# Later heads of the first group on a spare bank, second group's staged reads first, mirrored tokens and late sums moved

## What is computed

```
h = tokens(x)             # |FFT| of (poly+gauss), sigmoid mask, soft minimum
xn = layernorm(h)
q, k, v = xn @ Wq, xn @ Wk, xn @ Wv        # 8 heads of 64
attn = sigmoid(q k^T * 8)                   # keys and queries of one signal
h = h + relu((attn v) @ Wo)
y = layernorm(h)
h = h + shared_mlp(y) + top2_of_4_experts(y)
```

## Time and profile before

| | us |
|---|---|
| three runs | 173.07, 173.97, 174.40 (median 173.97) |
| the profiled execution, whole | 172.75 |
| its span, first to last instruction | 170.9 |
| PE busy | 152.8 (89% of the span) |
| ACT busy | 113.2 (66%) |
| DVE busy | 109.2 (64%) |
| POOL busy | 53.1 (31%) |
| TensorE's mean granted clock | 0.97 of full |

### The profile page before, as it was taken

One profiled execution on the slowest core, in us unless ns is written; L12 is line 12 of the kernel. 1 busy time (PEld: TensorE's weight loads), 2 busy tenths in 40 slices (PEclk: granted clock), 3 DMA queues, 4 the chain that ended last, 5 costly groups with the idle time before them and its releaser, 6 DMA issues.

```text
span 170.9 us, 6658 instructions
## 1 busy us (share of the span) xinstructions
PE 152.8 (89%) x2826; PEld 92.0 (54%) x2826; DVE 109.2 (64%) x278; ACT 113.2 (66%) x155; POOL 53.1 (31%) x99
## 2 busy tenths in 40 slices
PE   7996858699495899999999999999999999999970
PEld 2576424354251466666676645454575664775760
DVE  2597989939631767777776576969458883544520
ACT  3698846779346389898988798737728546457410
POOL 4000058631399556464525244344300000000000
PEclk9999699999879699999999999999999999999999
DMA  3360000165956067475839600000001101001101
GB/s 111 110 209 0 4 0 0 66 180 163 249 137 180 6 167 195 126 192 163 230 106 244 171 0 4 4 4 0 4 6 29 32 4 30 24 14 30 26 23 44
DMA packets 14749, 14.03 MB, mean 82 GB/s; under 512 B 1300, under 2 KB 14492, under 8 KB 14656
## 3 DMA queue, kind: packets, MB, share of 16 engines
q1 hardware_dynamic: 14432, 13.42, 29.2%
q10 hardware_dynamic: 288, 0.20, 0.5%
HBM read 9.00 MB, written 4.60 MB: 80 GB/s over the span
## 4 chain that ended last, share of the span: by engine, by line
PE 69%; DVE 13%; ACT 7%; POOL 5%; issue 3%; DVEq 0%; ACTq 0%; POOLq 0%
PE ps L432 15%; PE ps L414 13%; PE ps L534 8%; PE ps L552 7%; PE ps L591 6%; PE ps L443 4%; PE ps L561 3%; PE ps L576 2%; PE ps L291 2%; POOL norm L1190 2%; PE ps L405 2%; PE ps L373 2%; ACT area L1069 1%; PE ps L362 1%; ACT square L1067 1%
## 5 line engine op out<-in xcount | busy, mean ns | idle before, releaser
L1134 ACT ACTIVATE probs<-ps 125x1000 f32<-125x1000 f32 x64 | 61.8, 1006 | 18.3 <-PE ps L414 15.2
L432 PE MATMUL ps<-probs,xn 124*32 124x250 f32 (+1 forms) x512 | 40.6, 387 | 1.5 <-DVE YS L919 1.5
L414 PE MATMUL ps<-YS,XT 128*32 128x500 f16 x448 | 35.8, 390 | 2.1 <-DMA YS<-y_stage 2.0
L432 PEld LDWEIGHTS ps<-probs,xn 124*32 124x32 f32 (+1 forms) x512 | 16.4, 112 | 14.6 <-issue 3.5
L1161 ACT ACTIVATE H2r<-ps,wf 128x500 f32<-128x500 f32 x16 | 10.8, 676 | 15.4 <-PE ps L552 15.4
L803 DVE COPY ZS<-ps 128x250 f32<-128x250 f32 x32 | 12.9, 412 | 11.8 <-PE ps L432 11.6
L1007 DVE TENSOR_TENSOR area<-H2r,ps 128x500 f32<-128x500 f32 x16 | 10.8, 674 | 10.1 <-ACT H2r L1161 8.5
L414 PEld LDWEIGHTS ps<-YS,XT 128*32 128x32 f16 x448 | 11.1, 99 | 11.2 <-ACT probs L1134 3.9
L552 PE MATMUL ps<-area,wf 128*64 128x500 f32 x64 | 16.7, 585 | 0.0
L1148 ACT ACTIVATE area<-ps,wf 128x500 f32<-128x500 f32 x24 | 15.9, 672 | 0.9 <-PE ps L534 0.9
L793 DVE CAST YP<-ps 128x500 f16<-128x500 f32 x14 | 9.5, 677 | 7.9 <-PE ps L373 7.9
(11 more groups left out here) (154 smaller groups left out, 249.1 us busy)
## 6 DMA issues: line engine op xcount, KB each, us to landing
YS<-y_stage SPq DMA_DIRECT2D x56, 125.0 KB, 3.1
y_stage<-YP SPq DMA_DIRECT2D x14, 250.0 KB, 3.2
tower_out<-res SPq DMA_DIRECT2D x8, 124.0 KB
wf<-wf_in SPq DMA_DIRECT2D x1, 648.0 KB, 5.5
wa<-wa_in SPq DMA_DIRECT2D x1, 512.0 KB, 5.0
ch<-ch_in SPq DMA_DIRECT2D x1, 160.0 KB, 4.6
area<-x_in SPq DMA_DIRECT2D x2, 70.3 KB
area<-x_in SPq DMA_DIRECT2D x1, 140.6 KB
```

The lines of the kernel that those rows point to most:

```text
L414: last = mm(ps[k0:k1, 2 * (n % 2) + j, 0:TG].rearrange("p (h n) -> p h n", h=2), XT[:, g % 3, (2 * bb + cj) * P + k0:(2 * bb + cj) * P + k ...
L432: last = mm(ps[R * hh:R * hh + R, 4 + bb, half * TB:(half + 1) * TB], xn[0:keys, 4 * g + 2 * bb + cj, :], probs[0:keys, n % 3, hh, :], sta ...
L1134: fn(probs[:, n % 3].rearrange("p (j h) n -> p j (h n)", j=2), ps[0:P, 2 * (n % 2):2 * (n % 2) + 2, 0:TG], ACT.Sigmoid, scale=SCORE_SCALE) ...
```

## The change

Four things change; no arithmetic is added or removed, and the transfers are the same ones.

**Spare bank.** Parts 4 and 5 of group 0 now go to bank 6, and group 1's two projections both to bank 7. So the first mixes, which write banks 4 and 5, wait for parts 2 and 3 alone. PE makes part 4 right after the projection `y_project(1, 0)`, ahead of `scores(1)`, and `y_project(1, 1)` and part 5 after the first mix. ACT and DVE follow that order. In new places `y_project(1, 1)` waits until DVE has emptied bank 7, and `y_project(2, ·)` until part 5 has left bank 6.

**Staged reads of group 1.** SP now does store, read, store, read for group 1, and only then the stores of group 2.

**Mirrored tokens.** POOL's two copies stand ahead of `inverse_deviation(16:20)`.

**Late sums.** DVE's `total(later, tok)` and `centre(later)` stand right after the first `z_take`, and `total(later, masked)` and `variance(later)` after the third.

```diff
-PARTS = ((0, 0, 2), (1, 0, 3), (0, 1, 4), (1, 1, 5), (2, None, 4), (3, None, 5))
+PARTS = ((0, 0, 2), (1, 0, 3), (0, 1, 4), (1, 1, 5), (2, None, 6), (3, None, 6))
@@ y_bank
-            return 7 if k == 1 and g in (1, 2) else 6
+            return 7 if g == 1 or (g, k) == (2, 1) else 6
@@ SyncE
-            send(1, 0)
-            send(1, 1)
-            read_back(1, 0)
-            for g in range(2, NG):
+            for k in range(2):
+                send(1, k)
+                read_back(1, k)
+            send(2, 0)
+            send(2, 1)
+            read_back(2, 0)
+            for g in range(3, NG):
                 send(g, 0)
                 read_back(g - 1, 1)
                 send(g, 1)
@@ y_project
-                if g == 1:
+                if g == 1 and k == 0:
                     pe.wait_ge(packed, 2)
+                elif g == 1:
+                    pe.wait_ge(y_lo, 1)
+                elif g == 2:
+                    pe.wait_ge(yd_lo, 6)
+                    pe.wait_ge(y_lo, 2)
                 else:
-                    pe.wait_ge(y_lo, 2 if g == 2 else 2 * g + k - 2)
+                    pe.wait_ge(y_lo, 2 * g + k - 2)
@@ y_part
-                if i >= 4:
-                    pe.wait_ge(yd_lo, i - 1)
+                if i == 5:
+                    pe.wait_ge(yd_lo, 5)
@@ mix
                 if n in (0, 2):
-                    pe.wait_ge(yd_lo, 5 + n // 2)
+                    pe.wait_ge(yd_lo, 3 + n // 2)
@@ TensorE, main loop
                 if n == 0:
-                    for k in range(2):
-                        y_project(1, k)
-                if n == 1:
-                    for i in (4, 5):
-                        y_part(i)
+                    y_project(1, 0)
+                    y_part(4)
+                if n == 2:
+                    y_project(1, 1)
+                    y_part(5)
@@ VectorE
             y_take(1, 0)
+            part_low(4)
             dve.wait_ge(square_pool, 1)
             total(third, masked)
             variance(third)
-            part_low(4)
             y_take(1, 1)
             part_low(5)
 
             z_take(0, 0)
+            dve.wait_ge(token_pool, 1)
+            total(later, tok)
+            centre(later)
             x_take(2)
             z_take(0, 1)
             y_take(2, 0)
             y_take(2, 1)
             z_take(0, 2)
-            dve.wait_ge(token_pool, 1)
-            total(later, tok)
-            centre(later)
+            dve.wait_ge(square_pool, 2)
+            total(later, masked)
+            variance(later)
             z_take(0, 3)
             x_take(3)
             z_take(1, 0)
             y_take(3, 0)
-            dve.wait_ge(square_pool, 2)
-            total(later, masked)
-            variance(later)
@@ ScalarE
-                if n in (1, 2):
-                    part_high(n + 3)
+                if n in (0, 2):
+                    part_high(4 + n // 2)
@@ GpSimd
             square_rows(later)
+            pool.wait_ge(token_pool, 1)
+            for rows in (slice(0, 16), later):
+                v.tensor_copy(tok[:, rows, NBIN:F], tok[:, rows, NBIN - 2:0:-1]).then_inc(mirrored, 1)
             inverse_deviation(slice(16, 20), later)
...
             inverse_deviation(slice(20, 32), later)
-            pool.wait_ge(dve1, dve1_at["token", third.start])
-            for rows in (slice(0, 16), later):
-                v.tensor_copy(tok[:, rows, NBIN:F], tok[:, rows, NBIN - 2:0:-1]).then_inc(mirrored, 1)
```

## The result

| | before | changed |
|---|---|---|
| median of the runs, us | 173.92 (4 runs, 173.07 to 174.40) | 167.86 (4 runs, 167.25 to 168.03) |
| profiled execution, us | 172.75 | 168.03 |
| its span, us | 170.9 | 166.2 |
| PE busy | 152.8 (89%) | 152.0 (91%) |

The ratio is 0.9651 with a 95% interval of 0.9606 to 0.9696: 3.5% faster, 6.1 us between the medians, where the profiled executions differ by 4.7.

A forecast was written before the change was run, and what follows sets the result against it. PE, full from 60 us, was taken as the bound, so the start of scores(24) decides. Mirrored copies, staged reads and spare bank: 172.75 - 4.18 - 2.5 - 0 = 166.1 us; with 1.22 to the median 167.3 us, range 165.0 to 170.0.

The forecast's parts named there:

- PE is the bound behind 60 us: From 60 us PE has no slack, so scores(24) starting T earlier ends the kernel T earlier.
- The mirrored copies: PE's 2.55 us wait before x_transpose(4) and the half clock behind it go: 4.18 us gained, bounds 2.1 to 4.18.
- The cover: DVE's moved sums fit its idle 2.04 us before x_take(2); h2 is ready for x_transpose(4) with about 0.7 us over.
- The staged reads: PE's 1.98 us wait before scores(12) goes, about 1 us appears before scores(16): 2.5 us gained, bounds -0.5 to 4.3.
- My low end of that landing: Group 2's first staged reads, (2,0), land at 46.8 us with each transfer price at its lowest; 49.1 expected.
- the second rival: SP's chain of stores and reads becomes the bound: staged reads gain 0.5 us or nothing, 169.3 to 170.3 us; chance 0.19.
- The first rival: Stores don't hold up the staged reads: 4.3 us gained there instead of 2.5, 165.5 us; chance 0.10.
- my two prices, 2.8 and 4.2: A last staged read lands after 2.8 us with nothing right behind it, 4.2 us when a store is.
- The clock: PE's expected idle time of 1 us before scores(16) leaves the granted clock alone, being shorter than the earlier waits.
- The spare bank: The 1.48 us stall moves from the first mix to scores(4): gain 0, bounds 0.3 lost to 0.5 gained.
- From the profiled execution to the median: The median of before lay 1.22 us above its profiled execution; 1.22 us was added to the forecast 166.1 us.

The follow-up runs named there:

- Experiment 1: The kernel before with only POOL's two mirrored copies moved ahead of the power of rows 16:20; 169.31 us, ratio 0.9755.
- experiment 8: The changed kernel with POOL's mirrored copies back in their old place, late sums still early; 168.93 us, ratio 0.971 to the kernel before.
- experiment 4: The changed kernel with SP's old order of stores and reads; 169.68 us, ratio 0.9779 to the kernel before, where the changed kernel beside it had 0.970.
- the pairing: The changed kernel with group 1 staged store, store, read, read; ratios 0.9557 and 0.9572 to the kernel before in two comparisons.
- experiment 2: The kernel before with only SP's new order of stores and reads; 173.72 us, ratio 1.0004.
- experiment 5: The first run of the pairing, the changed kernel with group 1 staged store, store, read, read; 166.40 us, ratio 0.9557 to the kernel before.
- experiment 6: The pairing plus y_project(3, 1) one score step later, against the kernel before: 165.45 us, ratio 0.9561; rerun 166.51 us beside the pairing alone at 166.15.

## Why the prediction was right, point by point

It said 167.3 us with a range of 165.0 to 170.0, and 167.86 was measured.

- **PE is the bound behind 60 us, so the time of `scores(24)` decides.** Right: 106.4 us from there to the end before, 106.5 after.
- **The mirrored copies, 4.18 us.** The trace gives 4.31 (12.89 to 8.58) for copies and sums together. Right in size. Experiment 1's 4.7 us between medians is no second proof of it: its profile has 2.8 us between `scores(16)` and `scores(24)`, where the wait of DVE takes something back, and 1.7 us from a clock that did not fall. The cover was as reckoned: DVE's sums lie where it was idle (35.02 to 36.95), and there remain 0.26 us of idle time before `x_take(2)`:

```profile
36.24 0.71 DVE L754 SCALAR_TENSOR_TENSOR mag<-norm,tok 125x528 f32<-125x528 f32 x1
37.21 0.42 DVE L793 COPY XT<-ps 128x500 f16<-128x500 f16 x1 [0.26 <-PE ps L365]
...
42.82 1.01 POOL L1198 TENSOR_TENSOR norm<-norm,half_neg 125x4 f32<-125x4 f32 x1 [2.64 <-DVE norm L764]
...
51.08 0.61 POOL L1215 TENSOR_TENSOR lnsq<-ln 125x256 f32<-125x256 f32 x1
```

POOL reached `lnsq` at 51.08, which is 49.9 plus the later start of 1.18: as forecast to the tenth. What the prediction did not see is that the two edits are largely substitutes for the 4 us (experiment 8).
- **The staged reads, 2.5 us.** The mechanism is right, the term too large. By the trace it is 2.00 - 0.59 = 1.4 us; by experiment 4, 1.4 to 1.9 us. The step that was off is the landing of a store behind four reads: I took 3.5 us for stores (1,1) and (2,0), and they took 4.0 and 4.4. The first cost nothing, since the store went out at 35.97 - 1.18 = 34.8 instead of 35.05 and the last read behind it took 2.9 us instead of 3.4: reads (1,1) landed at 43.0, where I had 43.5. The second went straight into group 2's reads, which landed at 51.08 - 1.18 = 49.9 where I had 49.1. (My low end of that landing, 46.8, was too low as well: store (2,0) can't go out before its data is ready at 40.2, which makes it 47.2.) The timeline of SP in the changed kernel:

```profile
31.52 0.60 SPq L250 DMA_DIRECT2D y_stage<-YP  x1
34.15 1.77 SPq L263 DMA_DIRECT2D YS<-y_stage  x4
35.97 0.54 SPq L250 DMA_DIRECT2D y_stage<-YP  x1
39.98 1.73 SPq L263 DMA_DIRECT2D YS<-y_stage  x4
41.75 1.18 SPq L250 DMA_DIRECT2D y_stage<-YP  x2
46.15 2.88 SPq L263 DMA_DIRECT2D YS<-y_stage  x4
```

and the landing of the store issued at 36.0:

```profile
L250 SPq DMA_DIRECT2D y_stage<-YP x1: 540/540/540, 36.0 to 36.0; - x1
DMA to landing us min/median/max: 4.0/4.0/4.0
```

Between 36.5 and 39.98, and again between 42.9 and 46.15, SP does nothing but wait for a store to land. That is the price of the new order which the second rival named, and PE's longest wait of the loop stands where it was forecast, with 1.86 us instead of 1. The two other orders bracket it: without the new order 1.4 to 1.9 us more, with the pairing about 1.5 less.
- **Reads delayed by stores.** The first rival, that a store issued later doesn't hold a read, is neither shown nor refuted. The Trainium skill (DMA: Bandwidth & Descriptors, Queues, rings and completion order), on which it leaned, has each engine take the descriptors of a ring in order. The last read (1,0), with a store right behind it, took 3.7 us, which speaks against the rival; the last read (1,1), with two stores right behind it, took 2.9, which is the price with none. In the second profile of the changed kernel the two took 2.8 and 2.9, and in experiment 4 the last read (1,0), with nothing right behind it, took 3.7. So my two prices, 2.8 and 4.2, can't be put down to a store right behind the read; what separates them stays open.
- **The clock.** I expected an idle time of 1 us to leave it alone. It was 1.86 and left it alone. That is luck as much as insight: the clock fell behind 1.98 and 2.65 us at `scores(12)`, but not behind 1.89 at the same place (experiment 1) nor behind 2.91 at `scores(16)` (experiment 8). I had argued that 1 us is shorter than either wait behind which it fell; the length alone doesn't decide. The rule of the Trainium skill that I set aside (TensorE: Matmul & The Clock Gate, HAM oscillation) puts all of these on the harmless side, and two of them were not.
- **The spare bank, 0.** Right in the main: the idle time moved to `scores(4)`, 0.83 us of it where 1.4 was forecast, and the gain by the traces is 0.1 to 0.2 us.
- **From the profiled execution to the median.** I added the 1.22 us by which the median of before lay above its profile. The changed kernel's median lay 0.2 us under its own profile. So the total came within 0.6 us partly because two things cancelled: the changed kernel's profile had lost 1.18 us ahead of the loop, and the 1.22 us that I had added did not recur. That is luck. Over all profiles but that at a clock of 0.75 the first scores begin between 27.09 and 28.60 us, and the changed kernel's first profile is the latest of them.

## What to carry to other kernels

When an engine is full behind some point, follow one number, when it gets to that point, and look for the wait that ends last ahead of it. A gain in front of a wait that ends at a fixed time is worth nothing until that wait is gone (experiment 2: 0.0 us alone; experiment 4: 1.4 to 1.9 beside the others, likely but not proven by time), so cost edits in pairs. In a list of dependent transfers, issue what is ready before what must wait for a landing: the second store ahead of the first reads was worth 1.5 us more than the change had. And before a difference between two profiles is put down to a low clock, find the first instruction that is late: here it stood ahead of the low clock.

## What the runs showed of the hardware

- The length of a wait alone doesn't say whether the granted clock falls. At `scores(16)` five profiles have waits of 1.40 to 2.91 us, and it stayed at 1.00 behind all of them. At `scores(12)` it stayed behind 1.89 and fell to 0.50 behind 1.98 and 2.65; at `x_transpose(4)` it fell behind 2.55 and 3.67. What sorts them isn't shown. A wait of 2 to 3 us must be costed with and without some 1.5 us of clock (6.07 us from `scores(12)` to `scores(16)` against 4.61).
- A stretch at 0.50 ahead of the loop was 6.7 us long in one profile and about half of that in another, and cost nothing in either: it took 21.9 us from ACT's first square to the first scores (22.0 at most in all profiles but the one at 0.75). Such a stretch over the first scores themselves, in the profiles of experiments 1 and 5, came with 12.30 and 11.86 us from `scores(0)` to `scores(8)`, where experiment 6's second profile of the pairing has 11.08. A single profile is not good for a difference of 1 us.
- The same 250 KB store in the same place of the same kernel landed after 3.2 us in one execution and 4.4 in another.
- In some executions PE stops within the 64 small matmuls of an attention output with nothing to wait for, as in the second profile of the changed kernel:

```profile
69.94 0.50 PE L451 MATMUL ps<-outW,ZS 128*32 128x64 f32 x19
70.76 0.81 PE L451 MATMUL ps<-outW,ZS 128*32 128x64 f32 x43 [0.32 <-issue]
```

The first profile has this attention output in one piece. In the six profiles with such a gap it takes 107.2 to 108.1 us from `scores(24)` to the end, in the seven without one 106.4 to 106.8 (the one at a clock of 0.75 aside). What fills the gap isn't shown; it was not tried.
